# A four-layer graph network: ACT's order in the node pass, and gathers by label without bounds or clearing

## The chip, the cores and the metric

One core of a Trainium2 chip runs the whole program in one launch. The metric is the device time in microseconds. The kernel before took 6267.40, 6253.86 and 6259.91 us in three runs, median 6259.91. Engines are named as the profile names them: PE (TensorE, its weight loads apart as PEld), DVE (VectorE), ACT (ScalarE), POOL (GpSimd), SP (SyncE, whose transfers stand as SPq).

## The reference, cut to what matters

100,000 nodes with 64 features, 50,000 edges sorted by destination. Four layers, each with a layer norm and a ReLU ahead of it and a residual behind it.

```python
h = relu(layernorm(x)); x = x + segment_sum(h[src] * edge_weight[:, None], dst)      # layer 0
h = relu(layernorm(x)); feat = h                                                     # layer 1
for step in range(4):
    msgs = (einsum('nd,khd->knh', feat, W) + b)[etype4, src]
    a = segment_sum(msgs, dst)
    r = sigmoid(i_r + h_r); z = sigmoid(i_z + h_z)        # i = a @ w_ih.T + b_ih, h = feat @ w_hh.T + b_hh
    n = tanh(i_n + r * h_n); feat = (1 - z) * n + z * feat
x = x + feat
h = relu(layernorm(x)); x = x + segment_sum(typed(concat(node_typed(h)[src], attr)), dst)   # layer 2
h = relu(layernorm(x)); x = x + attention(h, src, dst)                               # layer 3
```

A node that no edge points to has a = 0 in all four steps, so its state can be carried through them without any message.

## The kernel before, in words

**Stages.** The program has ten stages in order: the norm pass (`nodes_and_sum`, first loop), the node pass (`nodes_and_sum`, second loop, names with `nd_`), four GRU steps over the edges (`graph_round`, names with `step_`), the typed messages (`typed_round`), the logits, the softmax weights and the attended messages (names with `attend_`). A barrier stands between stages. Edges go in 49 chunks of 1024 (eight groups of 128, one per partition), nodes in blocks of 512 columns.

**The node pass.** It takes every node four times through the GRU without a message. Two chains of blocks run interleaved: one iteration of `loop_nodes` has eight slots q, and `slot(q)` gives the stage (q % 2), the turn t (q // 4) and the block u. In a slot PE makes p_r (L808), p_n (L811) and p_z (L813), then turns rows of the slot two before (`turn_out`, L420, into nd_p_out), which waits for DVE's new state nd_fT (L1102). ACT makes r (L950), z (L954), copies turned rows from PSUM to nd_ro for storing (`take_rows`, L970), and makes the candidate (tanh, L961). DVE makes r * h_n + i_n (nd_pre, L1083), the update (L1095, L1097, L1102) and adds the input x (L1109). There are no turned rows to copy in q1 and q7. From iteration 30 on (`summing`; phase B below, phase A before it) the layer 0 sum goes along: POOL gathers neighbours (L773), ACT weighs eight groups of 128 edges in q2 and in q6 (`weigh`, L1004, then two label copies L1006 and L1007), PE turns them, DVE scans (L1148, L1154) and makes nd_x1T (L1159), and ACT takes a square root in q0 and q4 (L996, which needs another activation table). Each engine runs its list in the written order; semaphores tie them together.

**Gathers by label.** In each of the four steps, in the typed round and in the logits round POOL issues 392 indirect DMAs of 128 rows (`gather_rows`, L385): eight per chunk into one of four buffers g[c % 4]. Each carries a bounds check against a register (count - 1) and drops an index beyond it. Ahead of the first, POOL waits for s_init, which DVE's clearing of g raises (L1379, L1631, L1762). In the typed round the same semaphore also tells SP that attr is cleared. L749 (x by destination), L764 (label slots), L773 (neighbours in the node pass) and L1982 (the output's scatter) are indirect DMAs with functions of their own.

Of the kernel before, what the change touches and what calls it, by code (L numbers as in the profile page):

```python
# [16 lines left out]
C = 49  # L17
# [8 lines left out]
ROWS = EP + NP_  # L26
# [3 lines left out]
TURN = 30  # L30
BIG = 1e30
EPS = 1e-5
RING = 4
# [15 lines left out]
def live(c, count):  # L49

    return not isinstance(c, int) or 0 <= c < count


def is_below(n, count):

    return isinstance(n, int) and n < count


def is_last(n, count):

    return isinstance(n, int) and n == count - 1


def landed(c, h, k):

    return 8 * k * (c - h) + 16 * k
# [306 lines left out]
    release(nc, sems)  # L373


def gather_rows(nc, pool, table, idx, g, s_init, s_read, s_g, count=ROWS):

    limit = pool.to_reg(count - 1)
    pool.wait_ge(s_init, 1)
    for c in range(C):  # L380
        if c >= RING:
            for s, per_chunk in s_read:
                pool.wait_ge(s, per_chunk * (c - RING + 1))
        for j in range(8):
            nc.gpsimd.indirect_dma_start(  # L385
                out=g[:, c % RING, j, :], out_offset=None, in_=table,
                in_offset=bass.IndirectOffsetOnAxis(ap=idx[:, 8 * c + j:8 * c + j + 1], axis=0),
                bounds_check=limit, oob_is_err=False).then_inc(s_g[c % RING], 16)


class Names:
# [11 lines left out]
    def sem(self, name):  # L403
        self.sems.append(self.nc.alloc_semaphore(f"{self.tag}_{name}"))
        return self.sems[-1]
# [54 lines left out]
def nodes_and_sum(nc, m):  # L460

    GR = 16
    with ExitStack() as ctx:
        a = Names(nc, ctx, "nd")
        sb, ps, sem = a.sb, a.ps, a.sem
# [22 lines left out]
        g = sb("g", [P, 2, 8, HW])  # L488
# [79 lines left out]
        def window(j, b):  # L568
            return 2 * (j - TURN) + b
# [209 lines left out]
        def _(pe):  # L779
# [94 lines left out]

            def turn_messages(c, b):
                if live(c, C):
                    pe.wait_ge(s_w, c + 1)
                    if not is_below(c, 2):
                        pe.wait_ge(s_fr, c - 1)
                    settle(pe, s_tick)  # L880
                    turn(pe, p_s[b], w[:, b].rearrange("p j d -> p (j d)"), m.ident[:]).then_inc(s_t, 1)
# [46 lines left out]
        def _(act):  # L928
# [12 lines left out]
                    act.wait_ge(s_var0, j + 1)  # L941
                    nc.scalar.activation(st0[:, 2], st0[:, 1], ACT.Sqrt, bias=m.eps[:, 0:1], scale=1.0 / D).then_inc(s_dev0, 1)

            def gate(i, stage, t, u):
                n = 4 * i + 2 * t + u
                first = is_below(i, 1) and t == 0
                act.wait_ge(s_gr[stage], n + 1)
                if not first:
                    act.wait_ge(s_pre[stage], n - 1)
                nc.scalar.activation(rg[:, stage, u], p_r[:], ACT.Sigmoid, bias=m.bias[:, B_R:B_R + 1]).then_inc(s_r[stage], 1)  # L950
                act.wait_ge(s_gz[stage], n + 1)
                if not first:
                    act.wait_ge(s_chg[stage], 2 * (n - 1))
                nc.scalar.activation(zg[:, stage, u], p_z[:], ACT.Sigmoid, bias=m.bias[:, B_Z:B_Z + 1]).then_inc(s_z[stage], 1)  # L954

            def candidate(i, stage, t, u):
                n = 4 * i + 2 * t + u
                act.wait_ge(s_pre[stage], n + 1)
                if not (is_below(i, 1) and t == 0):
                    act.wait_ge(s_f[stage], n - 1)  # L960
                nc.scalar.activation(cand[:, stage, u], pre[:, stage, u], ACT.Tanh, bias=m.bias[:, B_IN:B_IN + 1]).then_inc(s_cand[stage], 1)  # L961
# [33 lines left out]
                    act.wait_ge(s_var1, c + 1)  # L995
                    nc.scalar.activation(st1[:, 2], st1[:, 1], ACT.Sqrt, bias=m.eps[:, 0:1], scale=1.0 / D).then_inc(s_dev1, 1)  # L996

            def weigh(c, b):
                if live(c, C):
                    act.wait_ge(s_g[b], landed(c, b, 8))  # L1000
                    if not is_below(c, 2):
                        act.wait_ge(s_t, c - 1)
                    for k in range(8):
                        ins_ = nc.scalar.activation(w[:, b, k], g[:, b, k, 0:D], ACT.Copy, scale=m.ew_t[:, bass.ds(8 * c + k, 1)])  # L1004
                    ins_.then_inc(s_w, 1)
                    nc.scalar.copy(m.lab_i[:, bass.ds(8 * c, 8)], g[:, b, :, D]).then_inc(s_lb, 1)  # L1006
                    nc.scalar.copy(m.sgn_t[:, bass.ds(8 * c, 8)], g[:, b, :, D + 1]).then_inc(s_lb, 1)  # L1007

# [7 lines left out]
            def body(j, summing):  # L1016
                one, two = j - 1, j - 2
                for q in range(8):
                    here = (two if q % 2 else one, *slot(q))
                    if live(here[0], NI):  # L1020
                        gate(*here)
                    stage, t, u = slot((q + 6) % 8)
                    i = (two if stage else one) - (1 if q < 2 else 0)
                    if live(i, NI) and not (stage == SECOND and t == 1):
                        take_rows(i, stage, t, u)
                    if live(here[0], NI):
                        candidate(*here)
                    if summing and q % 4 == 0:
                        deviation_x1(window(j, q // 4 - 1))
                    if summing and q == 2:  # L1030
                        take_f0_slots(window(j, -1), 1)
                    if summing and q == 6:
                        take_f0_slots(window(j, 0), 0)
                    if not summing and q in (1, 5):
                        take_x0(j, q // 4)
                    if q in (3, 4) and live(j, NI):
                        take_f0(j, q - 3)
                    if summing and q % 4 == 3:
                        square_x1(window(j, q // 4), q // 4)
                    if summing and q == 2:  # L1040
                        weigh(window(j, 1), 1)
                    if q == 6 and (summing or is_last(j, TURN)):
                        weigh(window(j, 2), 0)

            act.wait_ge(s_init, 1)
            loop_pairs(act, norm)
# [145 lines left out]
def graph_round(nc, m, step):  # L1192

    last = step == 3
    with ExitStack() as ctx:
# [17 lines left out]
        p_r, p_z, p_n, p_i = ps("p_r"), ps("p_z"), ps("p_n"), ps("p_i")  # L1213
        if last:
            x1T = sb("x1T", [P, 2, L])
        s_init = sem("init")
        s_tick = sem("tick")
        s_g = [sem(f"gathered{q}") for q in range(RING)]
        s_mask = [sem(f"masks_loaded{h}") for h in range(2)]
# [51 lines left out]

        @block.gpsimd
        def _(pool):
            gather_rows(nc, pool, m.tab[step], m.lab_i, g, s_init, [(s_t, 1)], s_g)

        @block.tensor
        def _(pe):
# [98 lines left out]

        @block.vector
        def _(dve):
            nc.vector.memset(g[:], 0.0).then_inc(s_init, 1)  # L1379

            def body(j, q):
                h = q % 2
                if live(j - 2, C):
# [50 lines left out]
def typed_round(nc, m):  # L1434

    with ExitStack() as ctx:
# [94 lines left out]

        @block.gpsimd
        def _(pool):
            gather_rows(nc, pool, m.h2, m.lab_i, g, s_init, [(s_gs, 1)], s_g)

        @block.tensor
        def _(pe):
# [89 lines left out]

        @block.vector
        def _(dve):
            nc.vector.memset(attr[:], 0.0)  # L1630
            nc.vector.memset(g[:], 0.0).then_inc(s_init, 1)  # L1631

            def body(j, q):
                h = q % 2
# [37 lines left out]
def logits_round(nc, m):  # L1672

    with ExitStack() as ctx:
# [8 lines left out]
        dot = sb("dot", [P, 2, 8, D])  # L1683
        hT = sb("hT", [P, 2, L])
        p_t = [ps(f"p_t{h}") for h in range(2)]
        s_init = sem("init")
        s_tick = sem("tick")
        s_g = [sem(f"gathered{q}") for q in range(RING)]
        s_own = [sem(f"own_loaded{h}") for h in range(2)]
# [29 lines left out]

        @block.gpsimd  # L1720
        def _(pool):
            gather_rows(nc, pool, m.h3, m.lab_i, g, s_init, [(s_hs, 1)], s_g)

        @block.tensor
        def _(pe):
# [33 lines left out]

        @block.vector  # L1760
        def _(dve):
            nc.vector.memset(g[:], 0.0).then_inc(s_init, 1)  # L1762

            def body(j, q):
                h = q % 2
                if live(j, C):
# [305 lines left out]
```

## Time and profile before

| | |
|---|---|
| median of three runs | 6259.91 us |
| profiled execution | 6255.21 us, span 6253.4 us |
| PE busy | 4126.8 us (66%) |
| DVE busy | 4263.6 us (68%) |
| ACT busy | 2817.3 us (45%) |
| POOL busy | 4215.3 us (67%) |
| DMA | 843 MB, mean 135 GB/s |

No engine is busy throughout: the stages have different bounds, so the shares of the whole span say little, and the views by stage and by wait are the ones to read. In the profile "busy" on POOL is the issuing of indirect DMAs; "idle before <-issue" is time in which an engine waits for nothing that the profile shows. A clock of 1.00 is 2.4 GHz, one of 0.5 is 1.2 GHz.

### The profile page before, as it was taken

The page shows a single profiled execution, that of the slowest core. Times are in us where ns is not written, and L with a number is a line of the kernel's source. Part 1 is how long each engine was busy: PE and PEld are TensorE (multiplying, and loading weights), DVE is VectorE, ACT ScalarE, POOL GpSimd, SP SyncE. Part 2 cuts the span into 40 slices and gives each one's busy share as a digit, 9 for nine tenths or more (in the row PEclk, how much of TensorE's full clock was granted, in tenths as well). Part 3 has the DMA queues.
Part 4 walks back from the last instruction along what each step waited for, and adds up shares of the span by engine and source line. Part 5 has one row for each costly group of instructions (what it writes and reads, how often), then busy time and mean ns, then how long its engine had stood idle before and what let it go on. Part 6 is the DMA issues. An engine that isn't in the chain of part 4 may idle for free. (4 is left out here: it accounts for less than half of the span.)

```text
span 6253.4 us, 69919 instructions
## 1 busy us (share of the span) xinstructions
PE 4126.8 (66%) x13088; PEld 2025.5 (32%) x13088; DVE 4263.6 (68%) x6225; ACT 2817.3 (45%) x4941; POOL 4215.3 (67%) x3977
## 2 busy tenths in 40 slices
PE   0019888987777759997997899799968860102221
PEld 0004444444434334443443444344434430001110
DVE  3868888988888857776776777677746554546431
ACT  0346666677776745554554555444433321110000
POOL 2877777753434467776775777677667767774777
PEclk9999999999999979998998999999989985555555
DMA  2986555455454544443443444354445542223331
GB/s 69 297 273 208 197 171 180 157 159 164 150 165 148 160 131 123 120 123 94 123 121 100 119 120 124 105 140 135 137 107 145 148 119 71 75 71 88 103 98 55
DMA packets 701774, 843.23 MB, mean 135 GB/s; under 512 B 183377, under 2 KB 339524, under 8 KB 701646
## 3 DMA queue, kind: packets, MB, share of 16 engines
q1 hardware_dynamic: 554684, 715.49, 35.2%
q0 software_dynamic: 129360, 125.36, 10.0%
q10 hardware_dynamic: 17602, 1.05, 0.2%
q14 instruction: 94, 0.77, 0.0%
q8 instruction: 34, 0.56, 0.0%
HBM read 420.11 MB, written 425.30 MB: 135 GB/s over the span
## 5 line engine op out<-in xcount | busy, mean ns | idle before, releaser
L385 POOL DMA_INDIRECT step_g<-f_rows,lab_i x1568 | 1649.1, 1052 | 604.5 <-issue 476.5
L773 POOL DMA_INDIRECT nd_g<-h_and_label,src_i x392 | 429.9, 1097 | 553.9 <-ACT sgn_t L1007 445.3
L1428 DVE COPY_PREDICATED step_p_m<-step_mask,step_wb 128x512 f32<-128x512 uint8 x588 | 411.9, 701 | 330.7 <-ACT step_wb L1373 300.3
L1334 PE MATMUL step_p_w<-step_gT,wT 128*128 128x512 f32 x1176 | 609.5, 600 | 6.2 <-ACT step_wb L1373 6.2
L749 POOL DMA_INDIRECT nd_xg<-in_x,dst_i x392 | 449.2, 1146 | 235.9 <-issue 119.1
L1982 POOL DMA_INDIRECT out<-attend_o,last_i x392 | 406.4, 1037 | 177.7 <-issue 119.1
L385 POOL DMA_INDIRECT typed_g<-h_rows,lab_i x392 | 405.8, 1035 | 172.1 <-issue 119.1
L764 POOL DMA_INDIRECT h_and_label<-slot,lab_at x392 | 430.9, 1099 | 128.8 <-issue 126.0
L385 POOL DMA_INDIRECT logits_g<-h_rows,lab_i x392 | 412.7, 1053 | 153.0 <-issue 119.1
L1373 ACT ACTIVATE step_wb<-step_p_w,bias 128x512 f32<-128x512 f32 x588 | 400.5, 681 | 131.6 <-PE step_p_w L1334 131.3
L1083 DVE SCALAR_TENSOR_TENSOR nd_pre<-nd_p_n,bias,nd_rg 128x512 f32<-128x512 f32 x392 | 293.4, 748 | 176.1 <-ACT nd_rg L950 150.7
L954 ACT ACTIVATE nd_zg<-nd_p_z,bias 128x512 f32<-128x512 f32 x392 | 268.5, 685 | 270.4 <-PE nd_p_z L813 265.2
L808 PE MATMUL nd_p_r<-nd_fT,wT 128*128 128x512 f32 x588 | 329.8, 645 | 85.7 <-ACT nd_rg L950 85.7
L420 PE MATMUL logits_p_t<-ident,logits_hs 128*128 128x128 f32 x196 | 53.3, 427 | 491.0 <-DVE logits_hs L1780 491.0
L420 PE MATMUL nd_p_out<-ident,nd_fT 128*128 128x128 f32 x1568 | 245.3, 280 | 136.8 <-DVE nd_fT L1102 134.4
L811 PE MATMUL nd_p_n<-nd_fT,wT 128*128 128x512 f32 x588 | 322.9, 633 | 0.0
L961 ACT ACTIVATE nd_cand<-nd_pre,bias 128x512 f32<-128x512 f32 x392 | 284.0, 725 | 86.1 <-DVE nd_pre L1083 85.4
L1321 PE MATMUL step_p_r<-step_aT,wT 128*128 128x512 f32 x392 | 220.8, 645 | 144.1 <-DVE step_carry L414 143.8
L420 PEld LDWEIGHTS nd_p_out<-ident,nd_fT 128*128 128x128 f32 x1568 | 188.1, 143 | 391.5 <-issue 391.5
L813 PE MATMUL nd_p_z<-nd_fT,wT 128*128 128x512 f32 x588 | 312.2, 614 | 0.0
L1398 DVE SCALAR_TENSOR_TENSOR step_pre<-step_p_n,bias,step_rg 128x512 f32<-128x512 f32 x196 | 147.1, 751 | 214.7 <-ACT step_rg L1361 214.7
L1102 DVE TENSOR_TENSOR nd_fT<-nd_dif,nd_cand 128x512 f32<-128x512 f32 x392 | 271.4, 692 | 25.8
(275 smaller groups left out, 9941.2 us busy)
## 6 DMA issues: line engine op xcount, KB each, us to landing
f_rows<-nd_ro SPq DMA_DIRECT2D x294, 256.0 KB, 3.9
h_rows<-nd_cen SPq DMA_DIRECT2D x98, 512.0 KB, 3.8
step_mask<-masks SPq DMA_DIRECT2D x392, 128.0 KB
step_fT<-f_turned SPq DMA_DIRECT2D x196, 256.0 KB
f_turned<-step_fn SPq DMA_DIRECT2D x147, 256.0 KB, 2.1
f_rows<-step_rows SPq DMA_DIRECT2D x147, 256.0 KB
h_and_label<-nd_hx SPq DMA_DIRECT2D x49, 528.0 KB
f_rows<-nd_h SPq DMA_DIRECT2D x49, 512.0 KB, 3.0
```

The lines of the kernel that those rows point to most:

```text
L385: nc.gpsimd.indirect_dma_start(out=g[:, c % RING, j, :], out_offset=None, in_=table, in_offset=bass.IndirectOffsetOnAxis(ap=idx[:, 8 * c + ...
L420: mm = pe.transpose(out[:, k * P:(k + 1) * P], rows[:, k * P:(k + 1) * P], ident)
L749: nc.gpsimd.indirect_dma_start(out=xg[:, c % RING, j * D:(j + 1) * D], out_offset=None, in_=m.ins["x"], in_offset=bass.IndirectOffsetOnAxi ...
L764: nc.gpsimd.indirect_dma_start(out=flat, out_offset=bass.IndirectOffsetOnAxis(ap=m.lab_at[:, t:t + 1], axis=0), in_=m.slot[:, t:t + 1], in ...
L773: nc.gpsimd.indirect_dma_start(out=g[:, c % 2, j, :], out_offset=None, in_=m.ht, in_offset=bass.IndirectOffsetOnAxis(ap=m.src_i[:, 8 * c + ...
L808: pe.matmul(p_r[:], lhsT=m.wT[:, HR, :], rhs=f, start=True, stop=True).then_inc(s_gr[stage], 1)
L811: pe.matmul(p_n[stage][:], lhsT=m.wT[:, HN, :], rhs=f, start=True, stop=True).then_inc(s_gn[stage], 1)
L813: pe.matmul(p_z[:], lhsT=m.wT[:, HZ, :], rhs=f, start=True, stop=True).then_inc(s_gz[stage], 1)
L1334: pe.matmul(p_w[:], lhsT=m.wT[:, WK + k, :], rhs=gT[:, h], start=True, stop=True).then_inc(s_w, 1)
L1373: nc.scalar.activation(wb[:, k - 1], p_w[:], ACT.Identity, bias=m.bias[:, B_K + k:B_K + k + 1]).then_inc(s_wb, 1)
L1428: nc.vector.copy_predicated(p_m[h][:], mask[:, h, k], wb[:, k - 1]).then_inc(s_sel, 1)
L1982: nc.gpsimd.indirect_dma_start(out=m.out, out_offset=bass.IndirectOffsetOnAxis(ap=m.last_i[:, 8 * c + k:8 * c + k + 1], axis=0), in_=o[:, ...
```

## The change: what it does

It has four parts. In the node pass ACT's `gate` is cut in two, and the copy of turned rows moves from behind the z sigmoid to between the r and z sigmoids. `weigh` is cut in halves: four of its eight activations are issued one slot earlier (q1 and q5), the other four and the label copies stay in q2 and q6; PE's turning of a chunk waits for both halves. The gathers by label lose their bounds check, the register and `oob_is_err=False`. The clearing of g goes in the steps, the typed and the logits round, and with it POOL's wait for it.

```diff
-def gather_rows(nc, pool, table, idx, g, s_init, s_read, s_g, count=ROWS):
-    limit = pool.to_reg(count - 1)
-    pool.wait_ge(s_init, 1)
+def gather_rows(nc, pool, table, idx, g, s_read, s_g):
...
             nc.gpsimd.indirect_dma_start(
                 out=g[:, c % RING, j, :], out_offset=None, in_=table,
-                in_offset=bass.IndirectOffsetOnAxis(ap=idx[:, 8 * c + j:8 * c + j + 1], axis=0),
-                bounds_check=limit, oob_is_err=False).then_inc(s_g[c % RING], 16)
+                in_offset=bass.IndirectOffsetOnAxis(ap=idx[:, 8 * c + j:8 * c + j + 1], axis=0)).then_inc(s_g[c % RING], 16)
...
-                    pe.wait_ge(s_w, c + 1)
+                    pe.wait_ge(s_w, 2 * c + 2)
...
-            def weigh(c, b):
+            def weigh(c, b, half):
                 if live(c, C):
-                    act.wait_ge(s_g[b], landed(c, b, 8))
-                    if not is_below(c, 2):
-                        act.wait_ge(s_t, c - 1)
-                    for k in range(8):
+                    if half == 0:
+                        act.wait_ge(s_g[b], landed(c, b, 8))
+                        if not is_below(c, 2):
+                            act.wait_ge(s_t, c - 1)
+                    for k in range(4 * half, 4 * half + 4):
                         ins_ = nc.scalar.activation(w[:, b, k], g[:, b, k, 0:D], ACT.Copy, scale=...)
                     ins_.then_inc(s_w, 1)
+                if live(c, C) and half == 1:
                     nc.scalar.copy(m.lab_i[...], g[:, b, :, D]).then_inc(s_lb, 1)
                     nc.scalar.copy(m.sgn_t[...], g[:, b, :, D + 1]).then_inc(s_lb, 1)
...
                     if live(here[0], NI):
-                        gate(*here)
+                        gate_r(*here)
...
                     if live(i, NI) and not (stage == SECOND and t == 1):
                         take_rows(i, stage, t, u)
                     if live(here[0], NI):
+                        gate_z(*here)
                         candidate(*here)
...
-                    if summing and q == 2:
-                        weigh(window(j, 1), 1)
-                    if q == 6 and (summing or is_last(j, TURN)):
-                        weigh(window(j, 2), 0)
+                    if summing and q in (1, 2):
+                        weigh(window(j, 1), 1, q - 1)
+                    if q in (5, 6) and (summing or is_last(j, TURN)):
+                        weigh(window(j, 2), 0, q - 5)
...
-            nc.vector.memset(g[:], 0.0).then_inc(s_init, 1)
```

On ACT, in the node pass without the sum, the kernel before has for slots q0 and q1 (rg and zg are r and z, p_out the turned rows, cand the candidate):

```order
L950 ACTIVATE nd_rg<-nd_p_r,bias 128x512
L954 ACTIVATE nd_zg<-nd_p_z,bias 128x512
L970 COPY nd_ro<-nd_p_out 128x512
L961 ACTIVATE nd_cand<-nd_pre,bias 128x512
L950 ACTIVATE nd_rg<-nd_p_r,bias 128x512
L954 ACTIVATE nd_zg<-nd_p_z,bias 128x512
L961 ACTIVATE nd_cand<-nd_pre,bias 128x512
```

and the changed kernel at the same place:

```order
L947 ACTIVATE nd_rg<-nd_p_r,bias 128x512
L971 COPY nd_ro<-nd_p_out 128x512
L955 ACTIVATE nd_zg<-nd_p_z,bias 128x512
L962 ACTIVATE nd_cand<-nd_pre,bias 128x512
L947 ACTIVATE nd_rg<-nd_p_r,bias 128x512
L955 ACTIVATE nd_zg<-nd_p_z,bias 128x512
L962 ACTIVATE nd_cand<-nd_pre,bias 128x512
```

The copy changed places with z in q0; q1 has no copy and is as before.

In the first iteration with the sum, ACT has from q5 on in the kernel before (w are the weighed neighbours, lab_i and sgn_t the label copies):

```order
L950 ACTIVATE nd_rg<-nd_p_r,bias 128x512
L954 ACTIVATE nd_zg<-nd_p_z,bias 128x512
L970 COPY nd_ro<-nd_p_out 128x512
L961 ACTIVATE nd_cand<-nd_pre,bias 128x512
L950 ACTIVATE nd_rg<-nd_p_r,bias 128x512
L954 ACTIVATE nd_zg<-nd_p_z,bias 128x512
L970 COPY nd_ro<-nd_p_out 128x512
L961 ACTIVATE nd_cand<-nd_pre,bias 128x512
L1004 ACTIVATE nd_w<-nd_g,ew_t 128x64 x8
L1006 CAST lab_i<-nd_g 128x8
L1007 COPY sgn_t<-nd_g 128x8
```

and in the changed kernel:

```order
L947 ACTIVATE nd_rg<-nd_p_r,bias 128x512
L971 COPY nd_ro<-nd_p_out 128x512
L955 ACTIVATE nd_zg<-nd_p_z,bias 128x512
L962 ACTIVATE nd_cand<-nd_pre,bias 128x512
L1006 ACTIVATE nd_w<-nd_g,ew_t 128x64 x4
L947 ACTIVATE nd_rg<-nd_p_r,bias 128x512
L971 COPY nd_ro<-nd_p_out 128x512
L955 ACTIVATE nd_zg<-nd_p_z,bias 128x512
L962 ACTIVATE nd_cand<-nd_pre,bias 128x512
L1006 ACTIVATE nd_w<-nd_g,ew_t 128x64 x4
L1009 CAST lab_i<-nd_g 128x8
L1010 COPY sgn_t<-nd_g 128x8
```

Half of the weighing stands one slot earlier, behind the candidate of q5; the copies again stand before z.

## Rows read from the trace of the kernel before

**Rows 1.** Windows: from:to, length, busy of PE PEld DVE ACT POOL, clock, DMA, GB/s.
```profile
451.00:1284.00 833.00, 748.15 (x2651) 386.26 (x2650) 724.95 (x1026) 565.64 (x946) 647.42 (x597) 0.99 0.55 181
1284.00:2261.00 977.00, 717.07 (x2597) 390.08 (x2595) 796.45 (x1169) 678.41 (x1374) 425.42 (x389) 0.91 0.52 161
2282.00:2846.00 564.00, 486.63 (x1372) 219.64 (x1372) 404.69 (x590) 280.37 (x442) 406.77 (x393) 0.97 0.40 115
```

**Rows 2.** The gathers' line: duration min/median/max, who waited for it (us, times).
```profile
L385 POOL DMA_INDIRECT step_g<-f_rows,lab_i x1568: 991/997/1517, 2284.4 to 4514.1; - x196
...
  ACT typed_sq L1592: 284.1, 49
  ACT logits_sq L1747: 211.7, 49
  PE step_p_t L420: 112.5, 60
```

**Rows 3.** Groups by line: busy us, mean ns | idle before, releasers.
```profile
L385 POOL DMA_INDIRECT step_g<-f_rows,lab_i x1568 | 1649.1, 1052 | 604.5 <-issue 476.5 <-DVE step_g L1379 127.9
...
L1321 PE MATMUL step_p_r<-step_aT,wT 128*128 128x512 f32 x392 | 220.8, 645 | 144.1 <-DVE step_carry L414 143.8
```

**Rows 4.** Timeline of POOL, us 643 to 645: start, duration, [idle before].
```profile
643.40 0.58 POOL L738 DMA_DIRECT2D x_of_dst<-nd_xg  x1
644.28 1.33 POOL L749 DMA_INDIRECT nd_xg<-in_x,dst_i  x1 [0.30 <-issue]
```

**Rows 5.** The output's scatter: duration min/median/max.
```profile
L1982 POOL DMA_INDIRECT out<-attend_o,last_i x392: 966/972/1827, 5717.4 to 6241.9; - x196
```

**Rows 6.** Timeline at the start of the logits round.
```profile
5124.87 1.76 DVE L1762 MEMSET logits_g<- 128x2048 f32 x1 [6.45 <-PEq L99]
5126.91 1.00 POOL L385 DMA_INDIRECT logits_g<-h_rows,lab_i  x1 [33.88 <-DVE logits_g L1762]
```

**Rows 7.** Timeline of one q0 and the r of q1 in phase A.
```profile
1006.16 0.69 ACT L954 ACTIVATE nd_zg<-nd_p_z,bias 128x512 f32<-128x512 f32 x1 [1.03 <-PE nd_p_z L813]
...
1008.32 0.63 PE L420 MATMUL nd_p_out<-ident,nd_fT 128*128 128x128 f32 x4 [2.27 <-DVE nd_fT L1102]
...
1009.06 0.59 ACT L970 COPY nd_ro<-nd_p_out 128x512 f32<-128x512 f32 x1 [2.21 <-PE nd_p_out L420]
...
1009.55 0.72 ACT L961 ACTIVATE nd_cand<-nd_pre,bias 128x512 f32<-128x512 f32 x1
...
1010.17 0.68 ACT L950 ACTIVATE nd_rg<-nd_p_r,bias 128x512 f32<-128x512 f32 x1
...
1010.97 0.75 DVE L1083 SCALAR_TENSOR_TENSOR nd_pre<-nd_p_n,bias,nd_rg 128x512 f32<-128x512 f32 x1 [0.20 <-ACT nd_rg L950]
```

**Rows 8.** Waits in phase A (508 to 1284 us): total us, times, longest.
```profile
ACT nd_ro L970 <- PE nd_p_out L420: 68.8, 57, 2.7
DVE nd_xb L1109 <- DMA nd_xb<-in_x: 46.7, 26, 2.2
```

**Rows 9.** The r sigmoids of phase A: count, durations, first and last start.
```profile
L950 ACT ACTIVATE nd_rg<-nd_p_r,bias x209: 667/687/712, 508.6 to 1283.9; 128x512 f32<-128x512 f32 x105
```

**Rows 10.** The r sigmoids of phase B.
```profile
L950 ACT ACTIVATE nd_rg<-nd_p_r,bias x153: 667/687/688, 1355.8 to 2206.8; 128x512 f32<-128x512 f32 x153
```

**Rows 11.** Timeline of phase B, from q6 to the r of the next q2.
```profile
1636.28 2.04 PE L808 MATMUL nd_p_r<-nd_fT,wT 128*128 128x512 f32 x2 [4.56 <-ACT nd_rg L950]
...
1644.27 2.02 ACT L1004 ACTIVATE nd_w<-nd_g,ew_t 128x64 f32<-128x64 f32 x8
...
1646.39 0.68 ACT L950 ACTIVATE nd_rg<-nd_p_r,bias 128x512 f32<-128x512 f32 x1
...
1647.11 0.75 DVE L1083 SCALAR_TENSOR_TENSOR nd_pre<-nd_p_n,bias,nd_rg 128x512 f32<-128x512 f32 x1 [0.68 <-ACT nd_rg L950]
...
1651.61 0.58 ACT L970 COPY nd_ro<-nd_p_out 128x512 f32<-128x512 f32 x1 [0.58 <-issue]
...
1656.48 1.12 PE L808 MATMUL nd_p_r<-nd_f0T,wT 128*128 128x512 f32 x2 [1.54 <-ACT nd_rg L950]
```

More of the change, by code:

```diff
@@ L942, in norm, with gate_r @@
                     nc.scalar.activation(st0[:, 2], st0[:, 1], ACT.Sqrt, bias=m.eps[:, 0:1], scale=1.0 / D).then_inc(s_dev0, 1)
-            def gate(i, stage, t, u):
+            def gate_r(i, stage, t, u):
                 n = 4 * i + 2 * t + u
@@ L950, in gate, with gate_z @@
                 nc.scalar.activation(rg[:, stage, u], p_r[:], ACT.Sigmoid, bias=m.bias[:, B_R:B_R + 1]).then_inc(s_r[stage], 1)
+            def gate_z(i, stage, t, u):
+                n = 4 * i + 2 * t + u
+                first = is_below(i, 1) and t == 0
                 act.wait_ge(s_gz[stage], n + 1)
@@ L1215, in graph_round @@
             x1T = sb("x1T", [P, 2, L])
-        s_init = sem("init")
         s_tick = sem("tick")
@@ L1273, in _ @@
         def _(pool):
-            gather_rows(nc, pool, m.tab[step], m.lab_i, g, s_init, [(s_t, 1)], s_g)
+            gather_rows(nc, pool, m.tab[step], m.lab_i, g, [(s_t, 1)], s_g)
         @block.tensor
@@ L1533, in _ @@
         def _(pool):
-            gather_rows(nc, pool, m.h2, m.lab_i, g, s_init, [(s_gs, 1)], s_g)
+            gather_rows(nc, pool, m.h2, m.lab_i, g, [(s_gs, 1)], s_g)
         @block.tensor
@@ L1629, in _ @@
         def _(dve):
-            nc.vector.memset(attr[:], 0.0)
-            nc.vector.memset(g[:], 0.0).then_inc(s_init, 1)
+            nc.vector.memset(attr[:], 0.0).then_inc(s_init, 1)
             def body(j, q):
@@ L1685, in logits_round @@
         p_t = [ps(f"p_t{h}") for h in range(2)]
-        s_init = sem("init")
         s_tick = sem("tick")
@@ L1721, in _ @@
         def _(pool):
-            gather_rows(nc, pool, m.h3, m.lab_i, g, s_init, [(s_hs, 1)], s_g)
+            gather_rows(nc, pool, m.h3, m.lab_i, g, [(s_hs, 1)], s_g)
         @block.tensor
@@ L1761, in _ @@
         def _(dve):
-            nc.vector.memset(g[:], 0.0).then_inc(s_init, 1)
             def body(j, q):
```

## Prediction

> **What bounds the kernel now.** I read the windows by stage first, then each stage's waits, and only there the timeline. No engine bounds the whole span. In step 0 PE is busy for 486.6 of 564 us, in phase A of the node pass for 748.2 of 833, and in phase B for 717.1 of 977, where the granted clock is 0.91 on average against 0.99 in A [rows 1].
>
> The rounds over the edges are paced by POOL. A gather takes 997 ns at the median, and ACT stood 284.1 us in the typed round and 211.7 us in the logits round for gathered rows, once for each of the 49 chunks; PE stood 112.5 us for them in all four steps together [rows 2]. Between gathers POOL waits for "issue" only, 0.30 us each (476.5 us for 1564), so with the mean of 1052 ns one gather comes every 1.35 us [rows 3]. The reader is to see that this gap is part of an indirect transfer: a direct one from the same engine takes 0.58 us, and the next indirect has its 0.30 ahead of it [rows 4].
>
> In phase A 209 r sigmoids lie between 508.6 and 1283.9 us, eight to an iteration: 26 iterations of 29.82 us [rows 9]. In phase B 153 lie between 1355.8 and 2206.8: 19 iterations of 44.8 us [rows 10].
>
> **No bounds.** 2352 gathers lose the check. What remains is the index list, the 128 rows and the landing. No transfer of this trace is indirect and unchecked, so the price is bounded by neighbours. From below: the direct one, 0.58 us without the gap, which would take 0.72 off a period of 1.30 [rows 4]. Nearer is another indirect transfer of 128 rows with the same check, the output's scatter, 972 ns at the median [rows 5], 25 below the gather's 997: forms differ by that much for reasons other than the check. From above I allow the mirror image, 25 ns dearer, since an unchecked form may take another path in POOL's program. I take 0, the value of the nearest row once its check is counted as the same, and keep both ends.
>
> What x ns less per gather is worth: in the typed and logits rounds POOL decides all of it, 0.392 us for each ns in each. In steps 0 to 2 other engines are close behind: POOL's chunk takes 8 x 1.35 = 10.8 us, PE's work per chunk is 486.6 / 49 = 9.9 [rows 1], and PE waits for DVE's carry 143.8 us over 196 chunks of four steps [rows 3], 0.7 per chunk. With all of that wait kept the chunk can come down to 10.6, 0.2 x 49 = 10 us per step; beyond that a cheaper gather waits for a free buffer. PE's 112.5 us are the ceiling over all four steps. I use 10 us per step for steps 0 to 2 and nothing for the last, where the node output goes along and PE has more to do.
>
> The Trainium skill, "GPSIMD Engine Reference", section 3.1 (side-by-side cycle accounting), puts data-dependent branching at about 12 cycles per element, with GpSimd at 1.2 GHz. Taken serially over 128 indices that is 1.28 us, more than the whole 0.997 us of a checked gather, so the trace rules that reading out. Spread over eight cores, 16 indices each, it would be 0.16 us per gather if the check branches: an estimate from that page, which by the prices above would make the sum about 155 us lower. No run here shows whether it branches. The sum goes by the rows.
>
> **No clearing.** At the start of the logits round DVE clears g for 1.76 us from 5124.87, and the first gather begins 0.28 us after its end [rows 6]. Without both, POOL can begin when the barrier lets it go, which is about when DVE begins: at most 1.76 + 0.28 = 2.0 us, and at least nothing, if POOL comes out of the barrier that much later than DVE. There are six such rounds, all with POOL at their front, so 0 to 12 us; I take 1.5 each, nearer to the row, -9. Beyond these starts DVE's clearing hides nothing and is hidden by nothing. That g holds old numbers costs no time.
>
> **The copy between r and z, phase A.** PE turns rows in a slot after p_z, so the copy can never be ready before z. In the q0 shown, z starts at 1006.16 while p_out waits for DVE until 1008.32; the copy starts at 1009.06, the tanh 0.49 later, r of q1 at 1010.17, and DVE's pre at 1010.97 waits 0.20 for that r [rows 7]. With the copy first, z stands behind it on ACT, and behind z stand the tanh and the next r: copy still at 1009.06, z at about 1009.55, tanh one z later (0.58 from start to start, less than its 0.69), r of q1 at 1010.75, and pre 0.55 later, since it already waits there. DVE is the engine that pulls the next input block, 26 waits of 1.8 us for nd_xb [rows 8], so a late pre delays the block after. The other copies in an iteration find rows that are turned already, or push a z behind which there is slack: ACT waited for p_out 57 times, two in an iteration [rows 8]. Bounds: nothing, if DVE's wait for its input takes the delay up, and 57 x 0.58 = 33 us if every such place pays. I take one place, 0.55 x 27 iterations (26 and the start) = +15, as pre there waits for ACT and for nothing else.
>
> **The same in phase B, and the halves of weigh.** Eight weighings take 2.02 us in one piece; behind them r starts at 1646.39, and pre at 1647.11 has waited 0.68 for it [rows 11]. Half a piece earlier, while ACT waits for PE anyway, brings that r 1.0 us forward and pre up to 0.68. But PE turns the message statistics behind nd_x1T there, and the next slots are PE's and DVE's, so I let 0.4 of it stand per iteration. Against it: in q0 the copy starts at 1651.61, behind it now z, then tanh, the table load, the square root and r of q1, for which PE's next p_r stands 1.54 us [rows 11]. That puts 0.5 us on the path. Per iteration -0.4 + 0.5 = +0.1, x 19 = +2; the ends are -0.68 x 19 = -13 and +0.5 x 19 = +10. The neighbours' gathers for weigh are issued a whole chunk ahead, so that half a weigh one slot earlier waits for none.
>
> **Sum.** 0 - 9 + 15 + 2 = +8 on the profiled execution's 6255.2 (span 6253.4 and 1.8 around it): 6263. Of the three runs shown the median lies 4.7 above the profiled time and the lowest 1.4 below; I name 6264 us. By the ends of the terms without the gather's (-12 to 0, 0 to 33, -13 to 10) most of it lies within 6245 to 6285.
>
> **Rivals.**
>
> *The gather gets cheaper.* For it: the check reads a register and compares every index, and POOL decides in two rounds outright. Against it: the 0.30 gap stands before an indirect transfer whatever it is, and the transfer's rows remain. At 25 ns: 2 x 9.8 + 3 x 10 (0.2 us of a chunk is 25 ns of eight gathers) = -50, with +8 some 6213. At 100 ns: 2 x 39.2 + 30 = -108, some 6155.
>
> *The node pass loses more (slower).* One mechanism: z behind a copy that waits for PE's turning, and everything on ACT behind z. It decides if both of an iteration's waits for p_out pay in phase A (+33), and 0.5 us in q0 of phase B with none of the halves' gain (+10): with -9, +34, some 6289. The point is whether pre in the second place, too, is released by ACT. Against it: in phase A DVE waits for a load 26 times, which gives time back.
>
> *The gather gets dearer.* At 25 ns: 2352 x 0.025 = +59 if every round pays; with +8 some 6320. Only the thought of another code path speaks for it.
>
> *The clock recovers in phase B.* At 1636.28 PE starts a p_r after 4.56 us of idleness and takes 2.04 us [rows 11]; a granted clock of 0.91 [rows 1] says that such stretches recur. If the halves shorten the idleness so that the clock stays at 2.4 GHz, an iteration is rid of the extra time of its slow matmuls: this p_r takes 0.9 us more than the 1.12 at 1656.48 [rows 11], and if the two behind it are as slow and half of it lies beside other work, 1.4 us, -26 over 19 iterations, some 6237 with the +8. The idleness, however, comes from ACT's square root and table loads, which stay.
>
> **How the numbers follow.** A measurement of this kernel tells 0.2% (12.5 us) from no change, so "same" is 6247 to 6272. Forecast 0.42 (same 0.31, slower 0.08, faster 0.03); cheaper gather 0.36 (faster 0.35, same 0.01); node pass loses more 0.13 (slower 0.12, same 0.01); dearer gather 0.05 (slower); clock 0.04 (faster). Together faster 0.42, same 0.33, slower 0.25. The range reaches to a gather cheaper by 100 ns and to the node pass's worst: 6155 to 6290; the forecast's own is 6245 to 6285.
>
> **What would show it.** In the trace after: the gather's median (997) and its 0.30; the first gather of a round against SP's first load; r to r over eight slots in phase A (30.4 expected, 29.8 if the copy is free) and phase B (44.9); in q0 of phase A copy, z, tanh and pre's wait for r at 0.75. A gather under 970 ns makes the forecast wrong downwards; phase A at 31 us or more makes it wrong upwards.

## The result, and the profile after

The changed kernel took 6197.83 us (median of 6196.56 to 6202.74), the kernel before 6263.65 beside it: ratio 0.9898, 95% interval 0.9881 to 0.9915, 1.0% faster. The profiled execution's span is 6194.8 us, 58.6 below that of before. One run of `e7_typed_dodge` below took 19705.66 us at a granted clock of 0.22 and is in no figure here.

Where it went, by stage, from the starts of each round's first gather (and of the r sigmoids for the node pass), so that a stage ends where the next begins; the logits stage holds the softmax weights too. The four columns on the right are kernels with one part of the change alone, told of below.

| us | before | after | no bounds | no clearing | copy moved | halves |
|---|---|---|---|---|---|---|
| node pass, 47 iterations | 1661.6 | 1673.4 | 1660.9 | 1660.0 | 1680.9 | 1661.5 |
| four steps | 2283.6 | 2260.0 | 2279.1 | 2276.1 | 2284.3 | 2282.0 |
| typed | 558.8 | 553.4 | 555.2 | 556.2 | 558.0 | 558.1 |
| logits | 590.5 | 549.7 | 549.3 | 590.2 | 590.6 | 591.1 |
| attended messages | 536.1 | 538.0 | 537.2 | 537.4 | 536.8 | 537.6 |

Of the 58.6 us, 40.8 are in the logits round. The steps' time differs between kernels that share their code: where the steps are unchanged they take 2282.0 to 2290.6 us (five kernels with the check and the clearing), and where both are gone 2260.0 to 2263.8 (five kernels), so a difference of a few microseconds there shows nothing. The gathers' line by source in the kernel after, answering to [rows 2]:

```profile
L383 POOL DMA_INDIRECT step_g<-f_rows,lab_i x1568: 938/944/1447, 2293.6 to 4485.2; - x196
...
L383 POOL DMA_INDIRECT logits_g<-h_rows,lab_i x392: 940/944/1361, 5107.1 to 5597.4; - x196
...
  PE step_p_t L417: 26.8, 19
...
  ACT typed_sq L1593: 277.7, 49
  ACT logits_sq L1746: 172.6, 49
  PE step_p_t L417: 79.7, 22
```

An unchecked gather takes 944 ns at the median against 997, 53 less. The first of the two PE rows is new: POOL itself now waits, 26.8 us in 19 places, for PE to free a buffer. The second is PE's wait for gathered rows, 112.5 us before [rows 2] and now 79.7. ACT's wait for rows fell by 39 us in the logits round but by 6 in the typed round. The groups by line show why: after, then the two rounds in the kernel before.

```profile
L383 POOL DMA_INDIRECT step_g<-f_rows,lab_i x1568 | 1562.2, 996 | 651.9 <-issue 471.0 <-POOLq L99 154.0 <-PE step_p_t L417 26.8
...
L383 POOL DMA_INDIRECT typed_g<-h_rows,lab_i x392 | 402.3, 1026 | 186.7 <-issue 119.2 <-POOLq L99 67.5
...
L383 POOL DMA_INDIRECT logits_g<-h_rows,lab_i x392 | 372.1, 949 | 151.1 <-issue 119.2 <-POOLq L99 31.9
...
L1324 PE MATMUL step_p_r<-step_aT,wT 128*128 128x512 f32 x392 | 219.7, 642 | 175.6 <-DVE step_carry L411 175.0
```

```profile
L385 POOL DMA_INDIRECT logits_g<-h_rows,lab_i x392 | 412.7, 1053 | 153.0 <-issue 119.1 <-DVE logits_g L1762 33.9
...
L385 POOL DMA_INDIRECT typed_g<-h_rows,lab_i x392 | 405.8, 1035 | 172.1 <-issue 119.1 <-DVE typed_g L1631 53.0
```

Medians agree over the rounds and means don't: some gathers are long. In the logits round the mean fell from 1053 to 949, 104 ns where the median fell by 53; in the typed round from 1035 to 1026, 9 ns. The timeline of the logits round before shows one long gather:

```profile
5412.10 0.69 DVE L1776 SCALAR_TENSOR_TENSOR logits_ho<-logits_own,logits_st 128x512 f32<-128x512 f32 x1
...
5412.71 0.69 DVE L1780 SCALAR_TENSOR_TENSOR logits_hs<-logits_g,logits_st 128x512 f32<-128x512 f32 x1
5412.86 1.41 POOL L385 DMA_INDIRECT logits_g<-h_rows,lab_i  x1 [0.30 <-issue]
5413.31 0.69 DVE L1783 TENSOR_TENSOR logits_dot<-logits_ho,wr 128x512 f32<-128x512 f32 x1
```

It starts 0.15 us into a DVE instruction that reads two tensors in SBUF and takes 0.41 us more than 0.997: until DVE is through. The same place after:

```profile
5401.39 0.69 DVE L1773 SCALAR_TENSOR_TENSOR logits_ho<-logits_own,logits_st 128x512 f32<-128x512 f32 x1
...
5401.99 0.94 POOL L383 DMA_INDIRECT logits_g<-h_rows,lab_i  x1 [0.30 <-issue]
5401.99 0.72 DVE L1777 SCALAR_TENSOR_TENSOR logits_hs<-logits_g,logits_st 128x512 f32<-128x512 f32 x1
...
5403.24 0.72 DVE L1782 TENSOR_TENSOR logits_dot<-logits_hs,wl 128x512 f32<-128x512 f32 x1
5403.24 0.94 POOL L383 DMA_INDIRECT logits_g<-h_rows,lab_i  x1 [0.30 <-issue]
```

Gathers now start every 1.25 us, and so do every second of DVE's instructions (5401.99, 5403.24): both start together, DVE's takes 0.03 longer, the gather nothing. In the typed round after they fall the other way, into the scans:

```profile
4804.86 1.27 DVE L408 TENSOR_TENSOR_SCAN typed_tot<-typed_mask,typed_carry,typed_msg 64x512 f32<-64x512 uint8 x1
4805.46 1.42 POOL L383 DMA_INDIRECT typed_g<-h_rows,lab_i  x1 [0.30 <-issue]
...
4806.34 1.28 DVE L410 TENSOR_TENSOR_SCAN typed_tot<-typed_mask,typed_carry,typed_msg 64x512 f32<-64x512 uint8 x1
4807.19 1.20 POOL L383 DMA_INDIRECT typed_g<-h_rows,lab_i  x1 [0.30 <-issue]
```

Two gathers of a chunk are held for 0.48 and 0.26 us there; in the kernel before it was about one, for 0.29, beside the norming (`typed_gs`), which also has two inputs in SBUF.

The start of the logits round after, answering to [rows 6]: DVE's clearing is gone, and POOL begins 0.67 us behind SP's first load; before, it began 2.54 behind (5126.91 [rows 6] against the load below).

```profile
5124.37 0.82 SPq L1710 DMA_DIRECT2D logits_own<-h_rows  x2
```

```profile
5106.44 0.82 SPq L1709 DMA_DIRECT2D logits_own<-h_rows  x2
5107.11 0.95 POOL L383 DMA_INDIRECT logits_g<-h_rows,lab_i  x1 [31.94 <-POOLq L99]
```

Waits in phase A after (508 to 1284 us), answering to [rows 8]:

```profile
ACT nd_ro L971 <- PE nd_p_out L417: 220.0, 155, 5.1
DVE nd_pre L1087 <- ACT nd_rg L947: 46.4, 75, 0.9
DVE nd_xb L1113 <- DMA nd_xb<-in_x: 27.0, 26, 2.3
ACT nd_zg L955 <- PE nd_p_z L810: 14.9, 52, 1.5
```

and two rows of the kernel before:

```profile
ACT nd_zg L954 <- PE nd_p_z L813: 150.2, 177, 2.5
DVE nd_pre L1083 <- ACT nd_rg L950: 2.6, 13, 0.3
```

ACT waits for turned rows 155 times, not 57, and z stands behind each of these waits. Most of that is not new time: z itself waited 150.2 us for its matmul before, and waits 14.9 now. What reaches DVE is new: its `nd_pre` waits for r in 75 places, not 13, and 43.8 us longer in all. DVE's wait for its input fell from 46.7 to 27.0 us, and its waits for PE's p_n and p_out from 18.8 to 6.2, so most of the delay was taken up there.

### The profile page after: what moved, and what is told of

It is laid out like the page before. It is cut to its first block and busy times, and to the rows that moved or that the text cites. A ratio compares the mean times of both kernels' runs of the same rounds, so it can differ in the third digit from the quotient of the medians.

```text
span 6194.8 us, 69939 instructions
## 1 busy us (share of the span) xinstructions
PE 4111.6 (66%) x13088; PEld 2021.2 (33%) x13088; DVE 4254.6 (69%) x6219; ACT 2805.4 (45%) x4941; POOL 4088.5 (66%) x3977
## 5 line engine op out<-in xcount | busy, mean ns | idle before, releaser
L383 POOL DMA_INDIRECT step_g<-f_rows,lab_i x1568 | 1562.2, 996 | 651.9 <-issue 471.0
L1429 DVE COPY_PREDICATED step_p_m<-step_mask,step_wb 128x512 f32<-128x512 uint8 x588 | 411.7, 700 | 347.4 <-ACT step_wb L1376 307.0
L383 POOL DMA_INDIRECT typed_g<-h_rows,lab_i x392 | 402.3, 1026 | 186.7 <-issue 119.2
L1979 POOL DMA_INDIRECT out<-attend_o,last_i x392 | 408.3, 1042 | 177.5 <-issue 119.1
L383 POOL DMA_INDIRECT logits_g<-h_rows,lab_i x392 | 372.1, 949 | 151.1 <-issue 119.2
L971 ACT COPY nd_ro<-nd_p_out 128x512 f32<-128x512 f32 x294 | 171.9, 585 | 386.0 <-PE nd_p_out L417 385.2
L1324 PE MATMUL step_p_r<-step_aT,wT 128*128 128x512 f32 x392 | 219.7, 642 | 175.6 <-DVE step_carry L411 175.0
```

The source lines that it names most:

```text
L383: nc.gpsimd.indirect_dma_start(out=g[:, c % RING, j, :], out_offset=None, in_=table, in_offset=bass.IndirectOffsetOnAxis(ap=idx[:, 8 * c + ...
L1429: nc.vector.copy_predicated(p_m[h][:], mask[:, h, k], wb[:, k - 1]).then_inc(s_sel, 1)
L1979: nc.gpsimd.indirect_dma_start(out=m.out, out_offset=bass.IndirectOffsetOnAxis(ap=m.last_i[:, 8 * c + k:8 * c + k + 1], axis=0), in_=o[:, ...
```

## The experiments

**Two theories.** G: the unchecked gather is cheaper, and the rounds in which POOL decides gain by it. H, formed on the traces of the first four runs: a gather that starts beside a DVE instruction with two inputs in SBUF is held until that ends, and the gathers' new period moves these meetings. The rivals are in the expectations.

**One part at a time.** `e1_no_bounds` leaves only the check out:

```diff
-    limit = pool.to_reg(count - 1)
...
-                bounds_check=limit, oob_is_err=False).then_inc(s_g[c % RING], 16)
+                ).then_inc(s_g[c % RING], 16)
```

> Only the bounds check goes (register, bounds_check, oob_is_err=False); clearing, waits and the node pass stay as before. Theory G (the unchecked gather is cheaper, and that is nearly all of the gain): gather median 944 ns against 997, steps 0 to 3 about 24 us shorter together, typed 3 to 8, logits about 39 shorter; ratio 0.9890, about 6194 us. Rival C (the gain comes with the clearing and its wait): median 944 but the kernel less than 25 us faster, 0.996 or above. Rival P (only phases shift, the gather itself is not cheaper): median stays 997.

Measured: 6211.20 us, ratio 0.9921 (0.9903 to 0.9939).

```profile
L384 POOL DMA_INDIRECT step_g<-f_rows,lab_i x1568: 938/944/1456, 2290.0 to 4498.3; - x196
...
L384 POOL DMA_INDIRECT logits_g<-h_rows,lab_i x392: 940/944/1463, 5124.3 to 5614.2; - x196
```

The gather's price and the logits round come out as G said, and P falls. But the expected ratio, 0.9890, lies outside the interval, and the steps, expected 24 us shorter, are 4.5 shorter (2283.6 to 2279.1): the cheaper gather alone does not give them their 23.6. POOL's group in the steps shows why a cheaper gather is worth little there:

```profile
L384 POOL DMA_INDIRECT step_g<-f_rows,lab_i x1568 | 1552.1, 990 | 680.0 <-issue 470.4 <-DVE step_g L1377 180.0 <-PE step_p_t L418 29.6
```

The gathers take 97 us less than the 1649.1 before [rows 3], but POOL waits 29.6 us for PE's buffers, for which it waits in no kernel with the check, and 180.0 instead of 127.9 ahead of the four first gathers.

`e2_no_clearing` keeps the check and drops the clearing of g and POOL's wait:

```diff
-    pool.wait_ge(s_init, 1)
...
-            nc.vector.memset(g[:], 0.0).then_inc(s_init, 1)
```

> Only the clearing of g and POOL's wait for it go; the bounds check stays. Theory G: first gather of each round 1 to 2 us earlier, six rounds, 6 to 12 us: ratio 0.9985 (6254). Rival C: 0.993 or below, with the logits round shorter by tens of us. Rival P: the gathers' long tails change (once per chunk, logits mean 1053 ns) though the median does not.

Measured: 6246.04 us, ratio 0.9982 (0.9971 to 0.9992); the six rounds together 10.4 us shorter by the table (7.5 + 2.6 + 0.3). As G said.

`e3_reorder` moves only the copy:

```diff
-                        gate(*here)
+                        gate_r(*here)
...
                         take_rows(i, stage, t, u)
                     if live(here[0], NI):
+                        gate_z(*here)
                         candidate(*here)
```

> Only the copy moves between r and z. Theory N (z behind a copy that waits for PE's turning): phase A 11 to 15 us longer over 28 iterations, phase B 0 to 10 longer, ratio 1.0020 to 1.0035 (6276 to 6285). Rival (the split is what costs): ratio 1.000.

Measured: 6279.26 us, ratio 1.0031 (1.0021 to 1.0041), the node pass 19.3 us longer: the order costs.

`e4_split` only halves weigh (four activations in q1 and q5, four in q2 and q6, PE waiting for `2 * c + 2`).

> Only weigh is cut in halves. Theory N: phase A unchanged, phase B 0 to 10 us shorter, ratio 0.9985 to 1.000. Rival (the split is what costs the node pass its 12 us): ratio 1.002.

Measured: 6258.17 us, ratio 1.0000 (0.9990 to 1.0010): nothing.

The four ratios multiply to 0.9934; the whole is 0.9898. The gap is about as large as the intervals allow (0.0018 on the first alone). By the table it is mostly in the steps: the four parts sum to 12.9 us there, the whole gains 23.6. Whether the cheaper gather and the missing clearing gain more together than alone, and why, was not tried.

**Back to the old order.** `e5_after_old_gate` is the changed kernel with the copy behind z again, as in the diff above, undone.

> The changed kernel with the copy back behind z; no bounds, no clearing and the halves of weigh stay. Theory N (the order of copy and z costs phase A 11 to 17 us and nothing else): ratio to before 0.9865 to 0.9880, about 6180 us, phase A back at 832 us. If the parts add up as measured alone (0.9921 x 0.9982 x 1.000): 0.9903. Rival (the order also bought something elsewhere): no faster than the changed kernel, 0.9898 or above.

Measured: 6193.12 us, ratio 0.9888 (0.9873 to 0.9903). The node pass is 1667.2 us in its trace, 6 below the changed kernel's; the interval overlaps the changed kernel's, so this run alone doesn't tell them apart. The gathers of this trace take 947 ns, not 944, and 0.3% of a node pass is 5 us. Three kernels below build on this one with the same node pass (`e7_typed_dodge`, `e11_typed_psum`, `e12_typed_attend_psum`): theirs takes 1661.3, 1660.6 and 1661.5 us, 12 below the changed kernel's 1673.4, as `e3_reorder` says from the other side.

**What the check costs.** `e8_check_as_error` leaves out only `oob_is_err=False`; `e9_no_register` leaves out only `bounds_check=limit` and the register.

> The kernel before with the bounds check and its register kept, but an index beyond it taken as an error, not dropped. If the dropping is what costs 53 ns: gather median 944. If the register or the comparing costs: 997. Between the two: both have a part.

> The kernel before without the bound and its register, but with an index beyond the table still dropped and not an error. If the register and the comparing with it cost the 53 ns (as e8_check_as_error, 1010 ns with both kept, suggests): gather median about 944. If the plain error form is needed as well: between 944 and 997.

Measured, one run each: 6276.73 and 6213.82 us. The gathers, first with the check as an error, then without bound and register:

```profile
L385 POOL DMA_INDIRECT step_g<-f_rows,lab_i x1568: 1004/1010/1527, 2286.7 to 4545.8; - x196
```

```profile
L384 POOL DMA_INDIRECT step_g<-f_rows,lab_i x1568: 938/944/1465, 2292.7 to 4493.5; - x196
```

1010 with the bound as an error, a value that no expectation had, 997 with it as a drop, 944 without a bound, dropping or not. The bound in a register is the 53 ns; which part of it (fetching the register, comparing) stays open, and so does why the error form is dearer.

**Who holds a gather.** `e6_logits_dodge` adds one useless instruction to the kernel before, to shift DVE's chain:

```diff
                                                    op0=ALU.max, op1=ALU.mult).then_inc(s_ho, 1)
+                    nc.vector.reciprocal(st[:, :, 3], st[:, :, 1])
```

> The kernel before with one useless DVE instruction more per chunk of the logits round (a second reciprocal, about 0.28 us, between the two normings, its result unused); the bounds check stays. Theory H (a gather that starts while DVE runs an instruction with two SBUF inputs is held until that ends; in the logits round the fourth gather of a chunk does so every time, 1399 ns instead of 997): the fourth gather starts beside the added instruction, its mean falls to about 1000 ns, the logits round is 15 to 20 us shorter, ratio 0.997. Rival L (the long gather is the queue's or the memory's doing): the long gathers stay, ratio 1.000. Rival D (DVE decides in this round): 14 us longer, 1.002.

Measured: 6261.54 us, ratio 0.9995 (0.9985 to 1.0004); the expected 15 to 20 us did not come. The timeline:

```profile
5405.97 0.69 DVE L1776 SCALAR_TENSOR_TENSOR logits_ho<-logits_own,logits_st 128x512 f32<-128x512 f32 x1
5406.58 0.25 DVE L1778 RECIPROCAL logits_st<-logits_st 128x16 f32<-128x16 f32 x1
5406.71 1.52 POOL L385 DMA_INDIRECT logits_g<-h_rows,lab_i  x1 [0.30 <-issue]
5406.74 0.63 DVE L1781 SCALAR_TENSOR_TENSOR logits_hs<-logits_g,logits_st 128x512 f32<-128x512 f32 x1
5407.28 0.68 DVE L1784 TENSOR_TENSOR logits_dot<-logits_ho,wr 128x512 f32<-128x512 f32 x1
...
5417.67 1.00 POOL L385 DMA_INDIRECT logits_g<-h_rows,lab_i  x1 [0.30 <-issue]
5417.74 0.66 DVE L1781 SCALAR_TENSOR_TENSOR logits_hs<-logits_g,logits_st 128x512 f32<-128x512 f32 x1
...
5418.92 0.68 DVE L1786 TENSOR_TENSOR logits_dot<-logits_hs,wl 128x512 f32<-128x512 f32 x1
5418.98 1.50 POOL L385 DMA_INDIRECT logits_g<-h_rows,lab_i  x1 [0.30 <-issue]
```

The added instruction moved the next by 0.16 us, not 0.28; the gather starts 0.03 ahead of the norming of the gathered rows (L1781) and is held almost to its end, 0.52. One chunk later it starts 0.07 ahead and is free, and the next, 1.31 later, falls into another of the four. This neither shows H nor breaks it: the shift was too small.

`e7_typed_dodge` adds a reduction of 0.69 us to the typed round of `e5_after_old_gate`:

```diff
+                    nc.vector.tensor_reduce(spare[:], g[:, q], AX.X, ALU.add)
                     nc.vector.scalar_tensor_tensor(out=gs[:, h], in0=g[:, q], scalar=0.0, ...)
```

> e5_after_old_gate with one useless DVE instruction more per chunk of the typed round (a reduction of the gathered rows, about 0.69 us, ahead of the norming, its result unused), which shifts the two scans against the gathers' starts. Theory H: of 0.73 us per chunk that the gathers are held by the scans, about 0.2 is left; the typed round 20 to 26 us shorter than in e5_after_old_gate, mean gather 950 to 970 ns instead of 1026, ratio 0.983 to 0.984. Rival L: the long gathers stay, ratio as e5_after_old_gate or slower. Rival D (DVE or PE decides in the typed round): no gain, with ACT's wait for rows gone.

Measured: 6188.57 us (median of three runs), ratio 0.9873 (0.9855 to 0.9891); the typed round 551.4 us against 552.7, no gain to speak of where 20 to 26 were expected.

```profile
4800.54 1.27 DVE L408 TENSOR_TENSOR_SCAN typed_tot<-typed_mask,typed_carry,typed_msg 64x512 f32<-64x512 uint8 x1
4800.67 1.89 POOL L383 DMA_INDIRECT typed_g<-h_rows,lab_i  x1 [0.30 <-issue]
...
4811.82 1.30 DVE L408 TENSOR_TENSOR_SCAN typed_tot<-typed_mask,typed_carry,typed_msg 64x512 f32<-64x512 uint8 x1
4811.86 0.94 POOL L383 DMA_INDIRECT typed_g<-h_rows,lab_i  x1 [0.30 <-issue]
```

A gather 0.13 us into a scan is held 0.95; one chunk later, 0.04 into it, not at all. Shifting in time is a gamble on hundredths of a microsecond, so the next runs take the cause away instead.

`e10_logits_psum` is the kernel before, check kept, with the second inputs of the four DVE instructions in PSUM:

```diff
+        p_st = ps("p_st")
+        inv = p_st[:, 0:16].rearrange("p (a b) -> p a b", a=2)
+        p_r, p_l = ps("p_wr"), ps("p_wl")
...
-                    ch.then(nc.vector.reciprocal(st[:, :, 2], st[:, :, 1]))
+                    ch.then(nc.vector.reciprocal(inv, st[:, :, 1]))
...
-                    nc.vector.tensor_tensor(dot[:, 0], ho[:], bc(m.wr[:], 1, [P, 8, D]), ALU.mult)
+                    nc.vector.tensor_tensor(dot[:, 0], ho[:], p_r[:].rearrange("p (j d) -> p j d", j=8), ALU.mult)
```

> The kernel before (bounds check kept); in the logits round the second inputs of DVE's four two-input instructions (the inverse deviations, the two weight rows) stand in PSUM, so that none has two inputs in SBUF; durations and order as before. Theory H (a gather that starts beside a DVE instruction with two SBUF inputs is held): no long gathers left in that round, mean 1053 to about 1000 ns, logits round 18 to 21 us shorter (590.5 to 571), ratio 0.9968. Rival L (queue or memory): long gathers stay, ratio 1.000. Rival B (DVE being busy at all holds a gather): long gathers stay.

Measured: 6239.04 us, ratio 0.9961 (0.9948 to 0.9975); the logits stage 568.3 us, 22.2 shorter. Its gathers, and the place of before's long one:

```profile
L385 POOL DMA_INDIRECT logits_g<-h_rows,lab_i x392: 992/997/1009, 5140.9 to 5649.7; - x196
```

```profile
5405.01 0.68 DVE L1787 SCALAR_TENSOR_TENSOR logits_hs<-logits_g,logits_p_st 128x512 f32<-128x512 f32 x1
5405.07 1.00 POOL L385 DMA_INDIRECT logits_g<-h_rows,lab_i  x1 [0.30 <-issue]
```

The longest of 392 gathers is 1009 ns, where it was 1521. The gather starts inside DVE's norming as before, the norming is as long, and nothing is held. Nor do the gathers merely miss DVE now: 46 of them start inside this norming, 48 inside the second product (`logits_hs` by `wl`) and 54 inside a reduction. H holds; L and B (DVE busy at all) fall.

`e11_typed_psum` is `e5_after_old_gate` with the typed messages in PSUM, where the scans read them:

```diff
-        msg = sb("msg", [P, 2, L])
-        p_c = [ps(f"p_c{h}") for h in range(2)]
+        p_c, p_m = ps("p_c"), ps("p_m")
...
-                    nc.scalar.copy(msg[:, h], p_w[0][:]).then_inc(s_m0, 1)
+                    nc.scalar.copy(p_m[:], p_w[0][:]).then_inc(s_m0, 1)
...
-                        nc.vector.copy_predicated(msg[:, h], mask[:, h, 3 + k], p_w[k][:])
+                        nc.vector.copy_predicated(p_m[:], mask[:, h, 3 + k], p_w[k][:])
```

> e5_after_old_gate with the typed round's messages in PSUM, where the scans then read them (one bank for them, one instead of two for the centred rows). Theory H: the scans no longer hold gathers; mean 1027 to 950 to 970 ns, typed round 20 to 28 us shorter than 552.7, ratio to before about 0.984. Rival P (PE or the single bank decides then): mean gather falls but the round gains under 10 us, ratio 0.987 to 0.989. Rival L: gathers as in e5_after_old_gate.

Measured: 6169.84 us, ratio 0.9855 (0.9840 to 0.9870); the typed stage 533.9 us, 18.8 shorter than in `e5_after_old_gate`, a little under the expected 20 to 28.

```profile
L383 POOL DMA_INDIRECT typed_g<-h_rows,lab_i x392 | 382.9, 977 | 186.7 <-issue 119.2 <-POOLq L99 67.5
...
4801.09 1.27 DVE L408 TENSOR_TENSOR_SCAN typed_tot<-typed_mask,typed_carry,typed_p_m 64x512 f32<-64x512 uint8 x1
4801.69 0.94 POOL L383 DMA_INDIRECT typed_g<-h_rows,lab_i  x1 [0.30 <-issue]
```

0.60 us into a scan, where the changed kernel's was held 0.48, the gather takes 0.94; of the 91 gathers that start inside the two scans none is held. The mean is 977 ns, above the expected 950 to 970; what is left is mostly the norming, whose two inputs stay in SBUF.

`e12_typed_attend_psum` does the same for the attended messages, where the output's scatter runs beside scans:

```diff
-        msg = sb("msg", [P, 2, L])
+        msg = [ps(f"msg{h}") for h in range(2)]
```

> e11_typed_psum with the attended messages in PSUM too, in the stage of the output's scatter. Theory H: of 26 us that the scatters are held there, the part by the scans goes (6 to 12 us), the part by the product of two SBUF rows stays: ratio 0.001 to 0.002 below e11_typed_psum. Rival L: as e11_typed_psum.

Measured: 6156.23 us, ratio 0.9830 (0.9816 to 0.9843), the fastest of all: 1.7% below the kernel before, and its interval lies clear of the changed kernel's.

```profile
L1973 POOL DMA_INDIRECT out<-attend_o,last_i x392 | 388.5, 991 | 177.7 <-issue 119.1 <-ACT attend_o L2004 58.6
```

The scatter's mean is 991 against 1042 after the change, the stage 518.2 us against 538.0: more than the 6 to 12 expected. The traces show why. In the changed kernel 95 scatters start inside a scan, and these are 21.5 us longer in all than 95 median ones; the expectation had put the scans' part too low. In this kernel 95 start inside a scan again and none is held; the 7.5 us that remain are beside the product of two SBUF rows.

The largest place of this kind is left as it was. In the steps of the changed kernel the 1568 gathers take 82 us more than as many median ones (996 against 944 ns), 74 of it in gathers that start inside the predicated copy of L1429, whose mask and data both stand in SBUF. No run took that away, and as POOL already waits for PE there, what it would be worth is not shown.

## Why the prediction was wrong

**No bounds: wrong.** The step that failed is "I take 0, the value of the nearest row once its check is counted as the same". That row had its check, so it could tell nothing of the check's price. `e1_no_bounds` and `e9_no_register` show 53 ns, inside the bounds, and the rival "the gather gets cheaper" is what happened. An estimate from the Trainium skill's figure for data-dependent branching ("GPSIMD Engine Reference", section 3.1) made 160 ns of it, if the check branches; the runs show a third of that, and not whether it branches.

**Its price by stage: the sum near by luck, the terms wrong.** With 53 ns the prediction's own prices give 20.8 us in each of the typed and logits rounds and up to 10 in each of three steps, 71.6 in all, and so 6191.6 us, 5 below the profiled 6196.56. But the logits round gained 41.2 in `e1_no_bounds`, the typed round 3.6, the steps 4.5 in all. The steps' term was too large because PE follows at once: POOL now waits for PE's buffer, and PE's wait for DVE's carry rose from 143.8 [rows 3] to 175.0 us (57 to 168 over the kernels with the check, 175 to 186 over those without). The two rounds' terms missed that a gather's length depends on where it starts. The prediction took the pace from the mean (1052) and the price from the median (997) [rows 2, 3] and did not ask what the difference is. In the logits round it is holding: 56 ns a gather before (22.0 us over 392) and 5 ns after (2.0 us), so the round gained 20.8 + 20.0 = 40.8 us, as measured. In the typed round holding grew from 38 to 82 ns, by 17.2 us, so 20.8 - 17.2 = 3.6 us are left, as in `e1_no_bounds` (5.4 with the clearing gone too). That this holding is DVE's doing and can be had without touching the check is shown by `e10_logits_psum` (-22.2). The Trainium skill names the conflict in "GPSIMD Engine Reference", section 1 (specifications): GpSimd's SBUF interfaces are shared with VectorE, with contention for DVE instructions with two SBUF inputs. The traces agree and give the size, 0.95 us for the gather of `e7_typed_dodge` shown above.

**No clearing: right.** -9 said, 10.4 measured; at the start of the logits round 1.9 us (2.54 to 0.67 behind SP's load), where 1.5 was taken.

**The copy between r and z: right in kind, near in part by luck.** For the order alone the prediction has +15 in phase A and 19 x 0.5 = +9.5 in phase B; `e3_reorder` shows 19.3 for the node pass. The count behind the +15 was wrong: not one place in an iteration pays but nearly three (pre waits for r in 75 places over some 26 iterations), 43.8 us more than before, and DVE's other waits gave back 32 of it.

**The halves of weigh: not shown.** The prediction took 19 x 0.4 = 8 us off for them. Alone they gave nothing (`e4_split`, 1661.5 us against 1661.6). The changed kernel's node pass is 7.5 below that of `e3_reorder`, from which the halves alone set it apart there, but kernels with one and the same node pass differ by nearly as much (1657.4 to 1664.3), so this stays open.

**The rivals.** The node pass did not lose the 43 us of the slower rival (11.8 and 19.3); the dearer gather and the clock's recovery didn't happen: phase B lasts as long as before (829.2 and 829.8 us for the last 19 of the 47 iterations; 827.8 to 841.5 in other kernels with the node pass of before), and the granted clock from 1284 to 2261 us is 0.90, where it was 0.91 [rows 1].

## What to carry to other kernels

When a queue of like instructions paces a stage, read its median and its mean apart: the gap is something that holds some of them, and a DVE instruction with two SBUF inputs beside POOL's indirect transfers is a suspect. Put one input in PSUM where a bank is free; don't try to dodge in time. A price for an operation's option can't come from rows that all have the option: where none is without it, say that the traces can't tell, and let the sum stand at neither end.

## What the runs showed of the hardware that was not expected

A gather that starts during a DVE instruction with two SBUF inputs is held until about 0.13 us before that instruction's recorded end (5412.71 + 0.69 = 5413.40, and 5412.86 + 0.41 = 5413.27), 0.19 for the scan above; one that starts together with it (5401.99) or 0.04 us into it (`e7_typed_dodge`) is not, and near that edge it goes either way (`e6_logits_dodge`: held 0.03 ahead, free 0.07 ahead). The holding goes one way: of 97 scans of the typed round in the kernel before, the 90 that start inside a gather take 1283 ns at the median, the others 1277. A reduction, or an instruction with one input in PSUM, holds nothing (148 gathers of `e10_logits_psum` start inside one, and its longest takes 1009 ns). And a bound given in a register makes a gather of 128 rows 53 ns longer as a drop, 66 as an error.
